# Input transposes ahead of the qkv products and a new order of the attention's stages, in a convolution-attention and mixture-of-experts block

## The reference

```python
# 1. convolution-attention branch on a layer norm over channels, added to x
u = ln_c(x)
qkv = einsum('bchw,oc->bohw', u, w_qkv)                  # 192 channels
dw = conv5x5(qkv, w_dw, groups=192, padding=2)           # depthwise
pw = einsum('bgihw,goi->bgohw', dw.reshape(24 groups of 8), w_pw)
ms = concatenate([qkv, pw], axis=1)                      # 16 heads of q, k, v, 8 each
q, k, v = relu(q), relu(k), [v, 1]
kv = einsum('bhnd,bhne->bhde', k, v)
out = einsum('bhnd,bhde->bhne', q, kv)
out = out[..., :-1] / (out[..., -1:] + 1e-15)            # quotients
x = x + batchnorm(einsum('bchw,oc->bohw', out, w_proj))
# 2. mixture of experts on a layer norm over channels, added to x
t = tokens(x); l = ln_t(t)
w = softmax(top2(l @ Wg + bg))
t = t + sum_e w[e] * (gelu(l @ W1[e] + b1[e]) @ W2[e] + b2[e])   # 8 experts, 64 -> 256 -> 64
```

## Time and profile before

| | |
|---|---|
| time, median of 3 runs | 123.15 us (122.67 to 123.2) |
| the profiled execution | 122.68 us |
| its span, first to last instruction | 121.0 us |
| granted TensorE clock | 1.00 |
| TensorE busy | 116.2 us (96%) |
| TensorE weight loads busy | 86.3 us (71%) |
| VectorE busy | 78.8 us (65%) |
| ScalarE busy | 70.1 us (58%) |
| GpSimd busy | 33.4 us (28%) |
| chain that ended last | PE 83%, DVE 9%, ACT 2%, issue 2% |
| of it, by line | L996 36%, L1293 18%, L1112 13% |

### The profile page before, as it was taken

One profiled execution on the slowest core, in us unless ns is written; L12 is line 12 of the kernel. 1 busy time (PEld: TensorE's weight loads), 2 busy tenths in 40 slices (PEclk: granted clock), 3 DMA queues, 4 the chain that ended last, 5 costly groups with the idle time before them and its releaser, 6 DMA issues.

```text
span 121.0 us, 3332 instructions
## 1 busy us (share of the span) xinstructions
PE 116.2 (96%) x1282; PEld 86.3 (71%) x1282; DVE 78.8 (65%) x267; ACT 70.1 (58%) x134; POOL 33.4 (28%) x51
## 2 busy tenths in 40 slices
PE   6999999999999889999999999999999999999991
PEld 5589956777798688977766876766766667666660
DVE  0489595753868998988991089976409055096972
ACT  4338799030596255378892894591973929729200
POOL 6727999990000003033250031000000000000370
PEclk9999999999999999999999999999999999999999
DMA  3579600000000000000000059921099590001001
GB/s 105 176 169 215 176 8 0 5 5 5 0 0 5 0 3 0 0 5 0 0 0 3 11 158 232 240 69 43 11 242 225 197 241 11 0 0 54 1 0 46
DMA packets 5460, 8.05 MB, mean 67 GB/s; under 512 B 1412, under 2 KB 3908, under 8 KB 5444
## 3 DMA queue, kind: packets, MB, share of 16 engines
q1 hardware_dynamic: 5344, 7.80, 25.0%
q10 hardware_dynamic: 100, 0.03, 0.2%
HBM read 7.24 MB, written 0.59 MB: 65 GB/s over the span
## 4 chain that ended last, share of the span: by engine, by line
PE 83%; DVE 9%; ACT 2%; issue 2%; POOL 1%; POOLq 1%; DVEq 0%
PE PS L996 36%; PE PS L1293 18%; PE PS L1112 13%; PE PS L1071 2%; DVE HEADWISE L898 2%; PE PS L1178 2%; PE PS L1081 2%; PE PS L1008 2%; PE PS L1217 1%; PE PS L1094 1%; PE PS L1203 1%; POOL XP L449 1%; PE PS L1024 1%; DVE XB L717 1%; PE PS L1248 1%
## 5 line engine op out<-in xcount | busy, mean ns | idle before, releaser
L573 ACT ACTIVATE MS<-PS,B 128x512 f32<-128x512 f32 x48 | 29.1, 689 | 7.2 <-PE PS L996 7.0
L996 PE MATMUL PS<-XS,W1H 128*128 128x512 f32 x64 | 26.5, 414 | 0.0
L996 PE MATMUL PS<-XS,W1L 128*128 128x512 f32 x64 | 25.3, 395 | 0.0
L1293 PE MATMUL PS<-MS,W 128*64 128x256 f32 x192 | 22.3, 383 | 0.0
L874 DVE SCALAR_TENSOR_TENSOR WY<-PS,B,HEADWISE 128x256 f32<-128x256 f32 x24 | 10.5, 480 | 14.8 <-PE PS L1293 14.5
L1293 PEld LDWEIGHTS PS<-MS,W 128*64 128x64 f32 x192 | 13.2, 137 | 8.5 <-ACT MS L573 1.5
L1112 PE MATMUL PS<-HEADWISE,BANDS 32*32 32x448 f32 (+2 forms) x480 | 15.9, 564 | 0.0
L996 PEld LDWEIGHTS PS<-XS,W1H 128*128 128x128 f32 x64 | 12.0, 188 | 4.8 <-ACT MS L573 1.0
L449 POOL TENSOR_TENSOR XP<-XP,WY 128x256 f32<-128x256 f32 x4 | 3.2, 808 | 41.1 <-DVE WY L924 40.8
L1112 PEld LDWEIGHTS PS<-HEADWISE,BANDS 32*32 32x32 f32 x480 | 10.9, 103 | 4.5 <-issue 1.2
L996 PEld LDWEIGHTS PS<-XS,W1L 128*128 128x128 f32 x64 | 12.0, 188 | 1.8
(11 more groups left out here) (135 smaller groups left out, 182.6 us busy)
## 6 DMA issues: line engine op xcount, KB each, us to landing
HEADWISE<-spread_dram SPq DMA_DIRECT2D x14, 256.0 KB, 4.9
W<-in_w_dram SPq DMA_DIRECT2D x3, 512.0 KB, 7.9
X<-in_x_dram SPq DMA_DIRECT2D x2, 256.0 KB, 3.1
HEADWISE<-spread_dram SPq DMA_DIRECT2D x4, 128.0 KB, 3.1
out_dram<-XP SPq DMA_DIRECT2D x4, 128.0 KB, 2.6
W<-spread_dram SPq DMA_DIRECT2D x2, 256.0 KB, 5.3
VEC<-in_vectors_dram SPq DMA_DIRECT2D x1, 132.0 KB
WQ<-in_w_qkv_dram SPq DMA_DIRECT2D x2, 48.0 KB, 2.8
```

Of the source, the lines that this page charges most:

```text
L573: act.activation(hidden(n), PS[:, h_bank(n), :], ACT.Gelu, bias=B1[:, k:k + 1]).then_inc(gelu_done, 1)
L996: return pe.matmul(PS[0:parts, bank, cols[0]:cols[1]], lhsT, rhs, start=start, stop=stop)
L1293: i = pe.matmul(PS[C * b:C * b + C, bank, at:end], W2[:, KC * e + k, :], hidden(KC * (E * s + e) + k)[:, N * b:N * b + N], start=begins an ...
```

## The change

1. The six warm-up products ahead of the qkv products go; `turn_input` (8 transposes of x) stands there, into banks 4 and 5 instead of 6 and 2.
2. ScalarE copies these to XB[:, 0] (`take_input`), one half before the square root and one after it. `residual` is gone.
3. VectorE sums XB over the channels (`input_means`) and centres it (`centred_input`) during the convolution; `centred_residual` now adds a centred bias to XB[:, 1]. The bias itself is added to XB[:, 0] by GpSimd, a new instruction.
4. The convolution's two inner loops change places: column group outside, row group inside. The four increments of `conv_ready` now come with the last four products.
5. After the convolution `turn_back` and `turn_back_q` are split by pair and dealt out among the other stages, pair 0 first; `second_heads(2)` goes from ScalarE to VectorE. The banks that they use change.
6. `attend` is split into `reciprocals` and `divide`, with other work between the two for pair 1.
7. The order of the stages changes on TensorE, VectorE and ScalarE until `xt(2)`; from `first_layer(0, 4)` on it is as before.

```diff
-        XT_BANKS = (6, 2)
+        XT_BANKS = (4, 5)
-        BACK_BANKS, BACK_Q_BANKS = (0, 1, 5, 7), (3, 4, 5, 2)
+        BACK_BANKS, BACK_Q_BANKS = (7, 0, 5, 4), (3, 1, 2, 3)
...
+            pool.wait_ge(bias_ready, 1)
+            pool.wait_ge(xb_centred, 2)
+            pool.tensor_tensor(XB[:, 0, :, :], XB[:, 0, :, :], BIAS[:, 0:1, :].broadcast_to([128, 16, C]), ALU.add)\
+                .then_inc(xb_whole, 1)
...
+            take_input(0)
             act.wait_ge(var_ready, 1)
             act.wait_ge(pads_set, 5)
             act.activation(DEV1[:, :], VAR1[:, 3, :], ACT.Sqrt, bias=EPS1[:, :]).then_inc(dev1_ready, 1)
+            take_input(1)
...
             relu_qt(0)
+            place_q(1)
+            place_q(2)
+            second_heads(3)
             relu_qt(1)
             copy_attt(0)
...
             for s in range(PAIRS):
                 first_v(s)
+            input_means()
             dve.wait_ge(w_high, 2)
...
+            centred_input()
             take_conv(0)
             normalisation()
+            centred_residual()
             take_conv(1)
-            second_heads(0)
-            residual()
...
-            warm_up(WARM_UPS_BEFORE_QKV, TILE_BANKS[1])
+            turn_input()
             pe.wait_ge(wqc_copied, 1)
...
+            def turn_back_q(s):
+                if s == 0:
+                    pe.wait_ge(cv_v, 4)
+                    pe.wait_ge(cv_s, 4)
+                if s == 3:
+                    pe.wait_ge(q_added, 1)
...
                 for m in range(2, len(taps)):
-                    for r in range(4):
-                        for c in range(4):
+                    for c in range(4):
+                        for r in range(4):
                             i = tap(0, r, c, 2 - c // 2, c % 2, *taps[m], False, m == len(taps) - 1)
-                        if m == len(taps) - 1:
-                            i.then_inc(conv_ready, 1)
+                            if c == 3 and m == len(taps) - 1:
+                                i.then_inc(conv_ready, 1)
...
-            turn_back()
-            pe.wait_ge(cv_v, 4)
-            turn_input()
-            turn_back_q()
+            turn_back(0)
+            turn_back(1)
+            turn_back_q(0)
+            turn_back(2)
```

More of the change, by code:

```diff
@@ L951, in _ @@
             variance(0)
-            attend(2)
-            read_kv(3)
+            reciprocals(1)
             scale(0)
             low(0)
+            divide(1)
+            read_kv(2)
+            read_kv(3)
             centre(1)
             whole(1)
-            attend(3)
             variance(1)
+            reciprocals(2)
+            divide(2)
+            scale(1)
+            low(1)
+            reciprocals(3)
+            divide(3)
             centre(2)
             whole(2)
-            scale(1)
-            low(1)
+            read_gates(0)
+            gaps(0)
             variance(2)
@@ L968, in _ @@
             low(2)
-            read_gates(0)
-            gaps(0)
+            places(0)
             variance(3)
-            places(0)
             softmax(0)
@@ L1043, in rs, with turn_input @@
                 i.then_inc(rs_ready, 1)
+            def turn_input():
+                for t in range(8):
+                    i = pe.transpose(PS[:, XT_BANKS[t // 4], 128 * (t % 4):128 * (t % 4) + 128],
+                                     X[:, 128 * t:128 * t + 128], IDT[:, :])
+                    if t % 4 == 3:
+                        i.then_inc(xt_ready, 1)
             def qkv(jp):
@@ L1064, in _ @@
             pe.wait_ge(rs_copied, 1)
+            pe.wait_ge(xb_copied, 1)
             qkv(2)
+            pe.wait_ge(xb_copied, 2)
             qkv(3)
@@ L1122, in conv_vk @@
                 for m in (0, 1):
-                    for r in range(4):
-                        for c in (0, 1):
+                    for c in (0, 1):
+                        for r in range(4):
                             tap(0, r, c, 2, c, *taps[m], m == 0, False)
@@ L1298, in _ @@
             kv(0)
-            pe.wait_ge(second_by_s, 2)
             qt(0)
+            turn_back(3)
+            turn_back_q(1)
+            turn_back_q(2)
+            num(0)
+            qt(1)
             kv(1)
-            pe.wait_ge(xb_ready, 2)
-            qt(1)
-            num(0)
+            attt(0)
+            turn_back_q(3)
+            proj(0)
+            num(1)
             kv(2)
-            num(1)
-            attt(0)
             qt(2)
+            kv(3)
+            xt(0)
             qt(3)
-            proj(0)
+            attt(1)
+            first_layer(0, 0)
+            proj(1)
             num(2)
-            attt(1)
-            kv(3)
-            proj(1)
+            first_layer(0, 1)
+            num(3)
+            first_layer(0, 2)
             attt(2)
-            num(3)
-            xt(0)
+            xt(1)
             proj(2)
-            first_layer(0, 0)
+            gate(0)
             attt(3)
-            first_layer(0, 1)
+            first_layer(0, 3)
             proj(3)
-            xt(1)
-            first_layer(0, 2)
-            gate(0)
-            first_layer(0, 3)
             xt(2)
```

148 lines of the change are left out of this document (72 added, 76 removed).

## The result

| | before | after |
|---|---|---|
| time, median of 4 runs | 123.18 us (122.67 to 123.28) | 127.62 us (127.44 to 128.04) |
| the profiled execution | 122.68 us | 127.44 us |
| its span | 121.0 us | 125.6 us |
| granted TensorE clock, mean | 1.00 | 0.986 |

After over before is 1.037, with a 95% interval of 1.034 to 1.041. The forecast was 124.2 us in a range of 122.7 to 125.3: the sign was right, the size was not.

What follows compares the result with a forecast made beforehand. TensorE, busy 116.2 of 121.0 us, was taken as the bound, through its issued work and gaps. Terms 0 - 0.6 + 1.9 = +1.3 us on 122.9 gave 124.2 us, range 122.7 to 125.3.

Steps and rivals of the forecast that it cites:

- Before the convolution, 0: Head of the kernel: input transposes replacing warm-ups change nothing in sum, between -0.1 and +0.3 us.
- The convolution, -0.6: Convolution loops: columns outside save 0.6 us through less ragged start and end, not a better steady rate; bounds -3.1 to +2.4.
- the ragged start: Start of the convolution: 29 weight loads per us at 17 us, expected to supply part of the 0.6 us gain.
- Rival 1: Convolution gains 1.3 to 3 us because queue neighbours use different row groups; decided from 38 loads per us; chance 0.25.
- The gaps behind it: After the convolution: new TensorE waits summing to 4.85 us, the largest 2.25 ahead of `xt(2)`.
- Either is finished some ten microseconds before `centre(0)` asks for it, so its value is 0: Under the convolution: GpSimd's new bias add, 0.8 or 3.2 us long, ends early enough to cost nothing.
- rival 4: Head of the kernel: without warm-ups the clock drops to 1.2 GHz, qkv products cost 2.87 us more, over 126; chance 0.03.
- The sign that I named for it: Head of the kernel: a granted clock under 1.00 around 8 to 15 us would show the forecast wrong.
- The rest of the +1.9: After the convolution: new gaps less old gaps and removed work, net +2.0, taken as +1.9 us; bounds +1.3 to +2.6.
- 4.85 - 1.8 = +3.05: After the convolution: 4.85 us of new TensorE gaps, less 1.8 us of old gaps that go.
- all behind it moves as a block: From `xt(2)` on: both programs issue the same instructions, so everything after it shifts by the same amount.
- The base of the forecast, 122.9: Whole kernel: average of four executions of before, 122.9 us, to which the +1.3 us was added.

Runs made afterwards that it cites:

- e4: The kernel before, with only the convolution's two inner loops swapped (column group outside, row group inside): 122.34 us, ratio 0.995.
- e6: The changed kernel, with GpSimd's whole bias add held until VectorE's four convolution copies are done: 125.27 us, ratio 1.019.
- e3: The changed kernel, with eight products of a zero tile in TensorE's idle time ahead of `xt(2)`: 126.14 us, ratio 1.025.
- e7: e4 plus early input transposes, row sums and centring under the convolution, and GpSimd's add held as in e6; old order after the convolution: 120.91 us, ratio 0.982.
- e12: e7 with the bias add moved from GpSimd to VectorE, behind `second_heads(0)`: 120.31 us, ratio 0.979.
- e2: The changed kernel, with GpSimd's bias add cut to one of 16 token tiles, the bias left out of the others: 125.66 us, ratio 1.019.
- e11: e4 with one more GpSimd instruction, a one-column memset of a tile that nothing reads: 122.53 us, ratio 0.995.

## Why the prediction was wrong

Its steps in their order:

- **Before the convolution, 0: right.** From the weight products (L1070) to the convolution 8.85 us passed, 8.89 before. Counted from the weight products, the square root starts 0.11 us later (1.90 us against 1.79), as forecast, and VectorE's scaling, which waits no more, 0.05 us sooner (3.22 against 3.27).
- **The convolution, -0.6: right in size, half right in the reason.** -0.58 in the ledger, -0.57 in e4 by itself, whose time bears it out (ratio 0.995). By the starts of the weight loads in both traces, the steady stretch keeps its rate, as I had it: 8.97 us from the 100th load to the 400th in each. But I had put a part of the gain at the ragged start, and there is none: the 120th load starts 4.20 us behind the first in both kernels, the 360th 11.30. All of it comes at the end, where the last load starts at 15.04 us before and at 14.47 now. Rival 1 falls with that. The changed kernel's stretch shows 36 loads, by the same view as the earlier trace rows:

```profile
22.00:23.00 1.00, 1.00 (x52) 0.75 (x36) 1.00 0.00 0
```

  The view also counts a load that began before the stretch; of loads that start within one microsecond there are 33 to 35 in both kernels, from 19 to 29 us. The same order took 15.3 or 15.6 us in different kernels, so the 0.6 is known to half its size.
- **The gaps behind it: right but for one.** 2.09 us for `xt(2)` (2.25 forecast), 0.51 and 0.25 for `proj(2)` and `proj(0)` (0.7 and 0.4), 0.38 for `attt(0)` and for `xt(0)` (0.3 and 0.4), 0.11 for `kv(0)` and 0.09 for `num(3)` (0.2 and 0.1). With the add held (e6) the first is 0.31, where 0.5 was forecast.
- **"Either is finished some ten microseconds before `centre(0)` asks for it, so its value is 0": the step that failed first.** The duration was fair (2.37 us between the bounds of 0.8 and 3.2), and the result was in fact early. But I asked only who waits for GpSimd's result, not who runs beside it. VectorE's instruction with two SBUF operands was held 1.9 us, and the copies 1.2 us; by e6 it costs 1.17 us of gap (1.48 - 0.31). The Trainium skill ("SBUF — State Buffer", Who interferes with whom) says that a VectorE instruction with two SBUF inputs contends with a GpSimd instruction that reads SBUF, that the second to issue is blocked until the first ends, and that a `tensor_reduce` never contends on this chip. The trace agrees on each: L716 held (2.11 us), L715 not (0.22 us), and with one operand in PSUM not either (0.42 us in e6). I had not weighed that page.
- **The clock, rival 4 at 0.03: the step that failed second.** I looked for a fall at the head, where warm-ups left, and gave it 0.03. The sign that I named for it, a clock under 1.00 at 8 to 15 us, did not come either. The fall came behind the 2.09 us gap that my own sum had found, and cost 1.6 us (e3). The trace of before has no gap over 0.53 us in this part, so it could not say what one of 2 us does; that called for a bound of its own on the term, twelve 512-column products at half rate, and I set none.
- **The rest of the +1.9: 0.6 short.** With both failures taken out the middle section is 5.25 - 1.17 - 1.6 = +2.5. Idle time makes +3.2 of it (4.1 in all in e6 against 0.95 before; 4.85 - 1.8 = +3.05 forecast) and the work -0.7, where I had -1.1. A third of the saving came back. 16 `turn_back` transposes, in groups of eight, four and four between other work, take 2.2 us from start to start after and 1.8 before, in one row; that covers the 0.4, though no run varies the grouping alone.
- **The end, +0.33: not foreseen.** I wrote that both programs issue the same instructions from `xt(2)` on and that all behind it moves as a block. 55.6 us did; the last 3 did not. It goes with GpSimd's new add (e7, e12), and the cause stays open.

The sum in one line: -0.6 + 1.9 + 1.2 + 1.6 + 0.6 + 0.3 = +5.0, which is the ledger's. The base of the forecast, 122.9, was also 0.3 us under the median of before that was measured beside the change (123.18).

## What to carry to other kernels

When work moves to an engine with idle time, look not only at who waits for its result but at what the other engines run beside it: a GpSimd pass over SBUF holds the first VectorE instruction with two SBUF operands until it ends, and all that stands behind it. A long wait that nothing covers costs TensorE more than itself, since the clock may fall behind it; where the order must change, check that each new gap of some 2 us has independent products ahead of it (two experts here: -3.2 us). And try the parts apart: the good ones of this change (early input transposes, centring under the convolution, the loops' order) give ratio 0.979 once the new order and the GpSimd add are left out.

## What the runs showed of the hardware

- GpSimd's add of 128x1024 took 2.37 us, VectorE's 1.23: four times the columns of the 0.81 us add of the earlier trace rows for 2.9 times the time.
- Behind a gap of 2.09 us on TensorE the clock fell from 2.4 to 1.2 GHz in 12 of 26 executions, for 3.4 us in each of the three that were profiled. With a gap of 1.20 us it did not, in four executions.
- Behind the last product, where TensorE has nothing more to do, the clock fell after 2.10 us of idle time in e2 and 2.15 in e7, and only after 3.04 in before. The stretches of e7, whose last product ends at 116.58 us:

```profile
118.00:119.00 1.00, 0.00 (x0) 0.86 0.38 131
119.00:120.00 1.00, 0.00 (x0) 0.50 0.00 0
```

- In the head the clock rose to 2.4 GHz between 4.2 and 7.0 us, differently from one execution to the next, and with it the start of the convolution wandered from 14.86 to 16.07 us.
- The 40 transposes in a row of the kernel before, 31.2 to 35.7 us, ran at a clock of 1.00, and so did the same 40 in e4 and e11.
- GpSimd's last add starts 1.19 us ahead of the last product's end with the extra add in the program, and 1.53 without, some 90 us behind that add; none of the runs says why.
